# Patch embedding of a vision-transformer layer: one FP32 product in place of three FP16 products

## The reference

```python
patches = patches.reshape(B, GRID * GRID, PATCH_DIM)          # 256 patches of 588 values
h = jnp.einsum('bpk,ek->bpe', patches, W) + b                 # 256 channels
h = h + attention(layernorm(h), wq, wk, wv, wo)               # 16 heads, 4 KV heads, causal, rotary
h = h + ffn(layernorm(h), clip_x, clip_down, w_gate, w_up, w_down)   # int8 grids, 704 wide
```

## Time and profile before

| what | value |
|---|---|
| time, median of 3 runs | 825.15 us (821.19 to 827.71) |
| the profiled execution | 827.79 us, with a span of 826.0 us from first to last instruction |
| TensorE matmuls busy | 669.9 us, 81% of the span |
| VectorE busy | 669.2 us, 81% |
| ScalarE busy | 591.2 us, 72% |
| GpSimd busy | 571.7 us, 69% |
| mean granted TensorE clock | 0.947 |
| start and first three images (no even rhythm yet) | 0 to about 90 us |
| images in an even rhythm | about 90 to 568 us |
| end of attention | about 568 to 660 us |
| feed-forward passes | about 660 to 826 us |

### The profile page before, as it was taken

The page is one execution under the profiler, slowest core; times in us unless marked ns, Lnnn a source line. Parts: engine busy times, 40 slices in busy tenths (PEclk is TensorE's granted clock), DMA queues, the critical chain, the costliest instruction groups (busy, mean ns, idle before and its releaser), DMA issues. The chain is left out here.

```text
span 826.0 us, 20673 instructions
## 1 busy us (share of the span) xinstructions
PE 669.9 (81%) x6706; PEld 384.2 (47%) x6706; DVE 669.2 (81%) x1052; ACT 591.2 (72%) x972; POOL 571.7 (69%) x561
## 2 busy tenths in 40 slices
PE   3577888888888888898888888889766459997894
PEld 2354555454555555555555555555332223332663
DVE  5954889888988898988889889898663359999894
ACT  4345778787788777778877877887665258886783
POOL 0455778787888788888878888886553148884363
PEclk9687999999999999999999999999897769999798
DMA  8235667667566666556656655665443112221499
GB/s 278 58 72 111 129 122 145 144 131 123 127 144 141 134 150 143 126 122 147 144 133 153 140 126 126 144 143 114 92 78 73 50 38 52 51 43 21 68 175 165
DMA packets 245383, 96.56 MB, mean 117 GB/s; under 512 B 222432, under 2 KB 240608, under 8 KB 245344
## 3 DMA queue, kind: packets, MB, share of 16 engines
q1 hardware_dynamic: 236896, 87.69, 48.7%
q0 software_dynamic: 8448, 8.39, 7.0%
HBM read 24.74 MB, written 16.78 MB: 50 GB/s over the span
## 5 line engine op out<-in xcount | busy, mean ns | idle before, releaser
L1205 DVE TENSOR_REDUCE act_all<-pair 128x4 f16<-128x1024 f32 (+1 forms) x192 | 234.4, 1221 | 21.6 <-PE pair L535 20.9
L978 POOL TENSOR_SCALAR_AFFINE_SELECT act_all<-act_all 128x512 f32<-128x512 f32 x128 | 104.5, 827 | 72.5 <-ACT act_all L829 72.5
L829 ACT ACTIVATE ffn<-pair 128x768 f32<-128x768 f32 x128 | 103.2, 806 | 67.3 <-PE pair L552 67.0
L484 PE MATMUL pair<-act_all 128*128 128x256 f16 (+1 forms) x960 | 118.2, 277 | 21.8 <-DVE act_all L1252 18.5
L978 POOL TENSOR_SCALAR_AFFINE_SELECT ffn<-ffn 128x512 f32<-128x512 f32 x128 | 94.0, 736 | 57.8 <-ACT ffn L829 57.0
L829 ACT ACTIVATE act_all<-pair 128x768 f32<-128x768 f32 x128 | 104.1, 813 | 30.7 <-PE pair L552 28.2
L484 PEld LDWEIGHTS pair<-act_all 128*128 128x128 f16 (+1 forms) x960 | 90.8, 99 | 41.5 <-issue 23.3
L1017 POOL TENSOR_TENSOR act_all<-act_all 128x1280 f16<-128x1280 f32 x31 | 81.7, 2636 | 18.3 <-ACT act_all L781 18.3
L550 PE MATMUL pair<-act_all 64*128 64x256 f16 x512 | 73.2, 282 | 18.9 <-DMA act_all<-act_all 10.9
L1191 DVE TENSOR_TENSOR act_all<-act_all 128x512 f16<-128x512 f32 x32 | 40.9, 1279 | 49.1 <-ACT act_all L822 49.1
L498 PE MATMUL pair<-act_all 128*128 128x384 f16 x384 | 76.4, 337 | 0.2 <-ACT act_all L767 0.2
(11 more groups left out here) (135 smaller groups left out, 1517.8 us busy)
## 6 DMA issues: line engine op xcount, KB each, us to landing
act_all<-x_t SPq DMA_DIRECT2D x32, 640.0 KB, 4.2
out<-act_all SPq DMA_DIRECT2D x32, 256.0 KB, 2.6
out<-ffn POOLq DMA_DIRECT2D x16, 512.0 KB, 6.9
act_all<-act_all SPq DMA_TRANSPOSE x192, 3.0
act_all<-w_down SPq DMA_DIRECT2D x1, 704.0 KB, 8.6
act_all<-w_emb SPq DMA_DIRECT2D x1, 640.0 KB, 4.0
ffn<-w_gate SPq DMA_DIRECT2D x1, 640.0 KB, 7.0
ffn<-w_up SPq DMA_DIRECT2D x1, 640.0 KB, 7.4
```

The costliest lines, as they stand in the source:

```text
L484: mm = pe.matmul(b, xs[0:k, sx, c, tb * P:(tb + 1) * P], we[0:k, sw, c, :], start=(c == 0 and (sx, sw) == PARTS[0]), stop=(c == KC - 1 and ...
L829: act.activation(probs[i // 4][:, o:o + 2, 0:3, :].rearrange("p h k s -> p h (k s)"), pair[1][:, :].rearrange("p (h c) -> p h c", h=2)[:, ...
L978: pool.affine_select(out=p, in_=p, pattern=[[0, 4], [1, P]], compare_op=ALU.is_ge, fill=0.0, base=0, channel_multiplier=-1).then_inc(maske ...
L1205: dve.tensor_reduce(to, pair[2][:, :].rearrange("p (k g t) -> p k g t", k=2, g=n_), AX.X, ALU.max).then_inc(unit_reduced, 1)
```

## The change

The patch product takes the loaded FP32 tiles as they are: 5 FP32 matmuls for a block of tokens, 10 for an image. The FP16 parts of patches and embedding weights, the ScalarE and GpSimd (and, at the start, VectorE) instructions that made them and their two semaphores are gone; `patch` waits for the load, and `next_x` waits for the patch product of the image that used the tile last.

```diff
-        x_parts = [part(2 * KC * TOKENS, FP16).rearrange("p (s c t) -> p s c t", s=2, c=KC) for _ in range(2)]
-        we = part(2 * KC * D, FP16).rearrange("p (s c e) -> p s c e", s=2, c=KC)
+        we = part(KC * D).rearrange("p (c e) -> p c e", c=KC)
...
-            sp.dma_start(raw_we, w_emb).then_inc(emb_loaded, 16)
+            sp.dma_start(we, w_emb).then_inc(emb_loaded, 16)
...
             def next_x(n):
 
-                sp.wait_ge(x_high_ready, n - 1)
-                sp.wait_ge(x_low_ready, n - 1)
+                sp.wait_ge(done["patch"], n - 1)
                 load_x(n % 2, n)
...
                 if x.known and z.n == 0 and tb == 0:
-                    pe.wait_ge(weights_split, 1)
+                    pe.wait_ge(emb_loaded, 16)
                 if tb == 0:
-                    pe.wait_ge(x_high_ready, z.n + 1)
-                    pe.wait_ge(x_low_ready, z.n + 1)
-                xs = x_parts[z.parity]
+                    pe.wait_ge(xt_loaded[z.parity], z.half * 16 + 16)
                 for c in range(KC):
                     k = P if c < KC - 1 else K_LAST
-                    for sx, sw in PARTS:
-                        mm = pe.matmul(b, xs[0:k, sx, c, tb * P:(tb + 1) * P], we[0:k, sw, c, :],
-                                       start=(c == 0 and (sx, sw) == PARTS[0]),
-                                       stop=(c == KC - 1 and (sx, sw) == PARTS[-1]))
+                    mm = pe.matmul(b, xt[z.parity][0:k, c, tb * P:(tb + 1) * P], we[0:k, c, :], start=(c == 0),
+                                   stop=(c == KC - 1))
...
-            def x_high(x):
-
-                v = x + 3
-                if v.known and v.n == 0:
-                    return
-                act.wait_ge(xt_loaded[v.parity], v.half * 16 + 16)
-                wait(act, done["patch"], v.n - 1)
-                act.activation(x_parts[v.parity][:, 0], xt[v.parity], ACT.Copy).then_inc(x_high_ready, 1)
...
-            act.wait_ge(emb_loaded, 16)
-            act.activation(we[:, 0], raw_we, ACT.Copy, scale=W_UNIT).then_inc(weights_high, 1)
-            act.wait_ge(xt_loaded[0], 16)
-            act.activation(x_parts[0][:, 0], xt[0], ACT.Copy).then_inc(x_high_ready, 1)
...
-                if (x + 4).exists():
-                    x_high(early)
...
-            def x_low(v):
-                if v.known and v.n == 0:
-                    return
-                pool.wait_ge(x_high_ready, v.n + 1)
-                pool.tensor_tensor(x_parts[v.parity][:, 1], xt[v.parity], x_parts[v.parity][:, 0],
-                                   ALU.subtract).then_inc(x_low_ready, 1)
...
-                if (x + 4).exists():
-                    x_low(early + 3)
...
-            weights_low(1, we, raw_we)
-            dve.wait_ge(x_high_ready, 1)
-            dve.tensor_tensor(x_parts[0][:, 1], xt[0], x_parts[0][:, 0], ALU.subtract).then_inc(x_low_ready, 1)
```

More of the change, by code:

```diff
@@ L160, in vit_layer @@
         xt = [part(KC * TOKENS).rearrange("p (c t) -> p c t", c=KC) for _ in range(2)]
-        x_parts = [part(2 * KC * TOKENS, FP16).rearrange("p (s c t) -> p s c t", s=2, c=KC) for _ in range(2)]
-        we = part(2 * KC * D, FP16).rearrange("p (s c e) -> p s c e", s=2, c=KC)
+        we = part(KC * D).rearrange("p (c e) -> p c e", c=KC)
         wqkv = part(2 * DC * QKV_COLS, FP16).rearrange("p (s c e) -> p s c e", s=2, c=DC)
         wo = part(2 * DC * D, FP16).rearrange("p (s c e) -> p s c e", s=2, c=DC)
[L168 to L171, removed]
+        raw = act_all[:, NG * A_COLS - DC * QKV_COLS - DC * D:NG * A_COLS]
+        raw_wqkv = raw[:, 0:DC * QKV_COLS].rearrange("p (c e) -> p c e", c=DC)
+        raw_wo = raw[:, DC * QKV_COLS:DC * QKV_COLS + DC * D].rearrange("p (c e) -> p c e", c=DC)
         h_parts = part(2 * TB * D, FP16).rearrange("p (s e) -> p s e", s=2)
@@ L258, in vit_layer @@
         weights_split = sem("weights_split")
-        x_high_ready = sem("x_high_ready")
-        x_low_ready = sem("x_low_ready")
         on_high_ready = sem("on_high_ready")
@@ L494, in project @@
                 if x.known and z.n == 0 and tb == 0:
-                    pe.wait_ge(weights_split, 3)
+                    pe.wait_ge(weights_split, 2)
                 for c in range(DC):
@@ L766, in embedded @@
                 fence(act)
-                act.activation(h_of(z), shared[JOBS.index(("patch", 0)) % 2][:, :],
-                               ACT.Copy, scale=1.0 / W_UNIT).then_inc(read["patch"], 1)
+                act.activation(h_of(z), shared[JOBS.index(("patch", 0)) % 2][:, :], ACT.Copy).then_inc(read["patch"], 1)
                 wait(act, h_turned[z.parity - 1], (z + -1).half * 16 + 16)
@@ L1154, in _ @@
             op.then_inc(centred, 1)
-            weights_low(2, wqkv, raw_wqkv)
-            weights_low(3, wo, raw_wo)
+            weights_low(1, wqkv, raw_wqkv)
+            weights_low(2, wo, raw_wo)
             dve.wait_ge(sig_ready, 1)
```

## The result

| what | before | after |
|---|---|---|
| time, median of 3 runs | 825.15 us (821.19 to 827.71) | 839.73 us (839.16 to 840.98) |
| ratio after / before | | 1.0185, 95% interval 1.0118 to 1.0253 |
| span of the profiled execution | 826.0 us | 838.0 us |
| period of an image, mean over 26 | 18.19 us | 18.59 us |
| TensorE, VectorE busy | 669.9, 669.2 us | 703.2, 645.8 us |

The change makes the kernel 1.8% slower, 14.6 us by the medians. TensorE works 33 us more and the three other engines 166 us less together, and neither sum shows in the time.

What follows compares the result with a forecast made beforehand. Bound by a loop of waits through several engines, not the busiest one. The period was to go from 18.19 to 18.33 us, +3.6 over 26, start -0.6: 830.8 profiled, 828 us as median; range 817 to 850.

Steps and rivals of the forecast that it cites:

- the gain and the price: Relief on the other engines was to cancel TensorE's 33% dearer patch product, leaving 828 us.
- TensorE's price: Patch product on TensorE: each block grows by 0.53 us, an image by 1.07, with weight loads hidden.
- Rival 2: FP32 weight loads in the open on TensorE: up to 3.4 us per image, 916 us; chance 0.07.
- The third loop as the new bound: Patch block, score pair 5, exponentials 5 and 6, score pair 7, back to first score pair: 18.33 us a period.
- The last leg of that loop: From exponential 6's end over score pair 7 and the projection to the first score pair: 0.16 + 0.38 + 1.15 us.
- rival 3: Loop through exponentials 5 and 6 and score pair 7 shorter than summed: period about 17.8, 814 us; chance 0.13.
- The length of that loop: Sum through exponentials 5 and 6 and score pair 7: 18.33 us, including 7.04 from first score pair to patch block.
- The start: First images: VectorE gains 1.8 us without `x_low`, the first product grows 1.07; net -0.6 us, bounds -1.8 and +1.5.
- The reason for `low`'s relief: VectorE's `low` no longer meets GpSimd's removed `x_low`: 1.18 us less per image.
- Rival 1: VectorE's `low` still meets a GpSimd instruction, mask 5 or 6: 28 us more, 853 us; chance 0.15.
- SyncE, `next_x`, ScalarE's `x_high` at nothing: No load is late on SyncE; without `x_high`, `on_low` starts up to 0.4 us earlier, exponential 5 no earlier.
- DMA loop: First score pair, patch block, score pair 4, `turn_max`, `turn_stack`, back to the score pair: 17.6 us a period.

Runs made afterwards that it cites:

- Experiment 6: Changed kernel with four of the five FP32 slices of the patch product, output not the reference's: 810.16 us, 0.9802 of the kernel before.
- Experiment 3: Changed kernel with masks 0 and 1 cut to 8 columns of one head: 827.14 us, 1.0014 of the kernel before.
- Experiment 1: Changed kernel with FP32 product, but ScalarE and GpSimd still make the FP16 parts, which nobody reads: 843.37 us, 1.0232 of the kernel before.
- experiment 2: Kernel before with its FP16 matmuls, split made for the first two images only and reused for all: 803.99 us, 0.9743 of the kernel before.
- experiment 5: Kernel before with score pair 5 issued ahead of the second patch block: 826.91 us, 1.0019 of the kernel before.

## Why the prediction came out as it did

The forecast was 828 us with a range of 817 to 850, most of it within 1% of before; the time is 839.73, slower by 1.8%. It lies in the range, but above the band of 821 to 834 that had most of the chance, and the gain and the price did not cancel. The new bound was named rightly; the sum was 11.7 us short. Of these, 6.8 us are the even periods (10.4 where 3.6 were forecast), 2.5 the start, -0.3 the end, and 2.6 the step from the profiled execution to the median, which was there in before and is nothing in after. By its steps:

- **TensorE's price: right.** A product of 256 columns was put at 427 ns; a block of ten records takes 2.36 us to the next instruction, 2.13 + 0.23. The forecast had 2.26: the first load of a block lies 0.10 us more in the open. Rival 2 did not occur. The Trainium skill ("TensorE: Matmul & The Clock Gate", weight-path perf modes) has fast weight load off for FP32 input; after's loads have a median of 190 ns, against 98 of FP16 ones, which agrees. Nine of ten are hidden within records that occupy the array 213 ns each (the forecast took 168 for a load, half of 335).
- **The third loop as the new bound: right,** and with it the signs that were named for it: score pair 7 waits for exponential 6, no DMA is a releaser at the first score pair, `low` is at 0.69 us. The period itself, 18.59, is above the named 18.2 to 18.4. Experiment 6 backs the bound: with 0.86 us less in two blocks a period of this loop is 0.86 us shorter.
- **The last leg of that loop: wrong.** The forecast led it from score pair 7 over the projection to the first score pair, 0.16 + 0.38 + 1.15 = 1.69 us. It took 1.41 and goes through ScalarE: 0.06 to score pair 7, 0.38 to exponential 7, its 0.81, and 0.16 to the first score pair, whose load names that exponential. The projection is done beside it; rival 3 had rightly doubted its 1.15.
- **The length of that loop: the step that was mis-sized.** It was 18.33 and is 18.62. Its terms in after: first score pair to patch block 7.44 (forecast 7.04), to score pair 5 5.31 (5.15), to exponential 5 0.38 (0.38), to the end of exponential 6 4.08 (4.07), then to the first score pair 1.41 (1.69). The 7.04 was carried over unchanged from before, and it holds a VectorE chain of its own: L1253, a reduction, L1174, another reduction, L1215. With masks 0 and 1 falling on L1253 and L1174 it grew by 0.40. Experiment 3 takes these meetings away and gives 0.45 us per period back. That the sum missed by only 0.29 us is in part luck: the leg that was taken too long (-0.28) hid as much of the two that were too short (+0.40 and +0.16).
- **The start: wrong in sign.** Forecast -0.6, measured +1.9. The gain was there (L1174 at 20 us takes 0.68 in place of 2.03 us), but the second image's product takes 6.17 us in place of 4.63: it starts 1.13 us earlier, at a granted clock of 0.50 that gives way to 1.00 only on the way (means of 0.73 and 0.74 over the two). At the third image's first reduction the two kernels were level. The 1.9 us come after that, 1.56 of them in the last period that isn't even (75.58 to 93.98, before 75.25 to 92.09), of which 1.23 lie between its first patch block and score pair 5; this was not tested by itself.
- **The reason for `low`'s relief: not needed, though its number was right.** The prediction credited it to the removal of `x_low`. Experiment 1 keeps `x_low` and has the same relief, so with the FP32 product it would have come anyway. What the removal gives in the FP32 kernel is 3.6 us, at the start; with FP16 products it gives 21 us (experiment 2).
- **Rival 1: its mechanism came, at another place.** It had VectorE meet a mask in place of `x_low`, at `low` and with masks 5 and 6, for 28 us. The meeting came with masks 0 and 1, at L1253 and L1174, for some 12 us. The prediction looked for meetings only at the instruction that was slow in before.
- **SyncE, `next_x`, ScalarE's `x_high` at nothing: right.** After has no wait for a patch load, and its DMA loop doesn't bind.

So of the 12.0 us between the profiled executions 10.4 are the third loop. With VectorE no longer held in the two meetings the kernel is level with before (experiment 3, 1.0014), as forecast. Left open: that the medians differ by 14.6 us and the profiled executions by 12.0, where before's runs spread over 821.2 to 831.6 us, so that the profiled one (827.79) need not be typical; what sets the uneven periods at the start; what each of the two meetings costs alone; and whether a place for `x_low` exists that meets nothing.

## What to carry to other kernels

In a pipeline of in-order queues, take a change's new distances and lay every instruction of VectorE against every one of GpSimd again, not only the one that was slow: a delay of a microsecond frees one pair and joins another, and both are as large as what the change was about. Shifts of 0.1 us count, since they decide which of the two engines waits. Measure the period of the loop and name all loops within 0.5 us of it; a fix on one is worth at most the distance to the next. And if work on an engine with slack is blamed for a stall, keep that work and change only the rest, as in experiment 1: it tells removal from shift. Check also that an experiment's number came about in the way that was expected: experiment 5's did not.

## What the runs showed of the hardware

- An FP32 matmul of 256 columns costs TensorE two records of some 213 ns at the 2.4 GHz level (granted clock 1.00), two clocks a column each: with one product less for each block (experiment 6) a block takes 1.92 us to the next TensorE instruction in place of 2.36. Its two loads (median 190 ns) are hidden except the first of a block, for which FP32 pays 0.10 us more than FP16 (0.23 us beyond the records against 0.13).
- VectorE instructions are held by GpSimd's even when tiny: an operation on two columns takes 0.16 us alone, 0.37 beside a mask of 0.64 us and 0.94 beside a subtraction of 1.40 us. The Trainium skill ("SBUF — State Buffer", two separate sides) calls the pair's port an exclusive lock held for a whole instruction; the end of L1246 (316.14) against that of the half `x_low` (316.12) agrees.
- It works both ways, and 0.1 us decides it: a mask that starts 0.11 us ahead of a VectorE instruction of 0.68 us holds it to 1.07 (after), one that starts 0.12 us behind it is held itself, to 0.62 us for 8 columns (experiment 3), and one that starts 0.02 us ahead still loses and takes 1.21 (before).
- A mask of 8 columns that met nothing took 0.19 us of GpSimd (experiment 3, 306.94) where that of 512 takes 0.64.
